# Hand-overs between feed-forward and attention: iterations one after another or woven turns

## What is computed

```python
def fp4_quant_dequant(x):  # blocks of 16 along the last dim
    scale = max(|x|) / 6, at least 1e-12
    q = GRID[searchsorted(MID, |x / scale|)] * sign(x) * scale
def ffn(x):                         # 128 -> 352 -> 128
    h = silu(fp4_linear(x, w_gate)) * fp4_linear(x, w_up)
    return fp4_linear(h, w_down)
def attention(X):                   # T 256, C 128, 16 heads of 8, causal
    A = softmax(mask(Q @ K.T / sqrt(8)))
    return (A @ V) @ Wo + bo
x = x + 0.5 * ffn(layernorm(x))
x = x + attention(layernorm(x))
x = x + 0.5 * ffn(layernorm(x))
```

## Time and profile before

| | us |
|---|---|
| median of 3 runs | 530.16 |
| the profiled execution, its own time | 529.12 |
| its span, first to last instruction | 527.3 |
| busy: PE, DVE, ACT, POOL | 424.6, 429.2, 295.7, 247.9 |

### The profile page before, as it was taken

One profiled execution on the slowest core, in us unless ns is written; L12 is line 12 of the kernel. 1 busy time (PEld: TensorE's weight loads), 2 busy tenths in 40 slices (PEclk: granted clock), 3 DMA queues, 4 the chain that ended last, 5 costly groups with the idle time before them and its releaser, 6 DMA issues.

```text
span 527.3 us, 12678 instructions
## 1 busy us (share of the span) xinstructions
PE 424.6 (81%) x3609; PEld 304.8 (58%) x3625; DVE 429.2 (81%) x1221; ACT 295.7 (56%) x716; POOL 247.9 (47%) x450
## 2 busy tenths in 40 slices
PE   0767777756758999999999998979874878877784
PEld 0435555544636777777777776647542555555564
DVE  5799999998688688888888887587446999999981
ACT  3245555555425677777777776445773355555542
POOL 3354345444514466666666664444542255434521
PEclk9989999999988999999999999789988799999998
DMA  7600000002553444444444445310000000000001
GB/s 213 185 0 3 0 0 0 0 0 66 149 144 102 107 133 134 135 126 122 119 124 129 131 131 134 106 29 5 4 1 1 11 11 20 20 20 19 12 20 31
DMA packets 30525, 35.50 MB, mean 67 GB/s; under 512 B 1683, under 2 KB 27283, under 8 KB 28179
## 3 DMA queue, kind: packets, MB, share of 16 engines
q1 hardware_dynamic: 30483, 34.99, 24.1%
HBM read 21.91 MB, written 10.49 MB: 61 GB/s over the span
## 4 chain that ended last, share of the span: by engine, by line
PE 39%; DVE 32%; issue 16%; ACT 4%; DMA 4%; POOL 2%; DVEq 1%; SPq 1%; ACTq 0%; POOLq 0%
PE bank L1045 7%; PE bank L1017 6%; PE bank L1072 6%; PE bank L1014 4%; DVE hq_amax L675 4%; DVE f_h L805 2%; PE bank L1076 2%; DVE hq_normed L686 2%; DVE hq_grid L709 2%; PE bank L994 2%; DVE hq_odd L692 2%; DVE fln_stats L714 2%; PE bank L956 2%; PE bank L1102 2%; DMA k_stack<-k_parts 2%
## 5 line engine op out<-in xcount | busy, mean ns | idle before, releaser
L836 DVE TENSOR_REDUCE nm<-bank 128x2 f32<-128x512 f32 (+1 forms) x192 | 127.9, 685 | 33.2 <-PE bank L1017 32.4
L618 ACT ACTIVATE probs<-bank 128x512 f32<-128x512 f32 x192 | 113.0, 601 | 64.1 <-PE bank L1045 62.6
L490 POOL TENSOR_SCALAR_AFFINE_SELECT probs<-probs 128x256 f32<-128x256 f32 (+1 forms) x192 | 93.2, 487 | 98.0 <-ACT probs L618 96.6
L1045 PE MATMUL bank<-q_stack,k_stack 75*128 75x256 bf16 (+1 forms) x512 | 75.5, 251 | 6.6 <-ACT probs L618 5.6
L1017 PE MATMUL bank<-k_stack,q_stack 72*128 72x256 bf16 (+1 forms) x512 | 74.8, 248 | 0.9
L924 PE MATMUL bank<-wguT,f_xT 128*128 128x352 f32 x128 | 54.8, 512 | 19.5 <-ACT f_xT L545 18.2
L956 PE MATMUL bank<-wdT,f_hT 128*128 128x128 f32 (+1 forms) x384 | 58.2, 290 | 14.1 <-ACT f_hT L563 14.1
L524 ACT ACTIVATE hq_magic<-hq_exps 128x704 bf16<-128x704 bf16 x32 | 25.3, 790 | 65.3 <-DVE hq_exps L695 65.3
L956 PEld LDWEIGHTS bank<-wdT,f_hT 128*128 128x128 f32 (+1 forms) x384 | 50.3, 200 | 18.7 <-ACT f_hT L563 18.7
L444 POOL TENSOR_TENSOR fln_mean_neg<-fln_mv,minus_one 128x2 f32<-128x2 f32 x32 | 6.3, 198 | 113.0 <-DVE fln_var_eps L725 113.0
L1014 PE MATMUL bank<-causal,ident_bf 128*128 128x256 bf16 (+1 forms) x176 | 54.5, 310 | 0.5 <-DVE nm L836 0.2
(11 more groups left out here) (122 smaller groups left out, 878.5 us busy)
## 6 DMA issues: line engine op xcount, KB each, us to landing
q_stack<-q_parts SPq DMA_DIRECT2D x16, 576.0 KB
k_stack<-k_parts SPq DMA_DIRECT2D x16, 576.0 KB
q_parts<-qk_parts SPq DMA_DIRECT2D x16, 192.0 KB, 2.1
k_parts<-qk_parts SPq DMA_DIRECT2D x16, 192.0 KB, 2.4
v_stack<-zeros_bf SPq DMA_DIRECT2D x1, 2048.0 KB, 10.3
k_parts<-qk_parts SPq DMA_DIRECT2D x16, 128.0 KB, 2.3
out_dram<-x_all SPq DMA_DIRECT2D x16, 128.0 KB, 1.8
q_stack<-nmT SPq DMA_DIRECT2D x16, 24.0 KB
```

The costliest lines, as they stand in the source:

```text
L490: nc.gpsimd.affine_select(out=v, in_=v, compare_op=ALU.is_ge, fill=0.0, base=0, pattern=[[0, heads], [1, P]], channel_multiplier=-1).then_ ...
L618: nc.scalar.activation(probs[:, c, :], ps[:, :], ACT.Exp, scale=SCALE).then_inc(done, 1)
L836: nc.vector.tensor_reduce(nm[:, j, h0:h0 + n], ps[:, :].rearrange("p (h k) -> p h k", h=n), AX_X, ALU.max, negate=True).then_inc(done, 1)
L1045: last = nc.tensor.matmul(ps[:, w * n:w * n + w], k_stack[0:SROWS, s, HG * g + h, k0:k0 + P], q_stack[0:SROWS, s, HG * g + h, q0:T], start ...
```

## The change

The two lists of digits are replaced by lists of turns. A turn names a feed-forward iteration, an attention iteration and an order of steps of both (`f.` for feed-forward's, none for attention's). Steps that don't exist for that iteration are passed over; one iteration may be spread over two turns (feed-forward 2 and 3 of the second hand-over), and assertions in `weave` hold that each step stands there once. The orders of SP's queue stay as they were.

```diff
--- before.py
+++ after.py
@@ -84,15 +84,48 @@
 
 
 FFN1_END = 13
-FFN_TO_ATT = [2, 2, 2, 2, 0, 1, 0, 1, 0, 1, 1]
-
-
-
-TOGETHER = """
-f.xT a.lnN f.lnS f.hq a.xT f.lnA f.lnE f.xq f.gu0 a.xTc f.xr f.hr a.third a.stack f.h0 a.qk f.hT0 a.c1 f.gu1
-a.lnS f.lnN f.hT1 a.split f.dn f.h1 a.lnA a.lnE a.bias a.c2 a.v
-""".split()
-ATT_TO_FFN = [0, 1, 0, 1, 0, 0, 0, 1, 0, 1, 0, 1]
+WARM = """
+third f.xT lnN f.lnS f.hq stack xT f.lnA f.lnE f.xq f.gu0 xTc f.xr f.hr f.h0 qk f.hT0 c1 f.gu1
+lnS f.lnN f.hT1 split f.dn f.h1 lnA lnE bias c2 v
+"""
+FIRST_SCORES = """
+third f.xT lnN f.hq stack xT f.gu0 xTc f.hT0 f.gu1 f.hr f.h0 f.h1 f.hT1 qk c1 S0 S1 f.dn S2 split S3 S4 lnS S5
+c2 S6 lnA S7 lnE S8 bias S9 v S10 S11
+"""
+FIRST_PROBS = """
+nmS third f.hT0 lnN nm S0 f.hT1 S1 xT f.hq xTc f.dn S2 stack f.hr qk ST0 c1 S3 ST1 S4 lnS S5
+ST2 split S6 bias lnA S7 ST3 c2 lnE S8 S9 v ST4 S10 S11
+"""
+FIRST_VALUES = """
+nmS ST5 S0 f.hT0 third  ST6 lnN S1 f.hT1  ST7 nm S2 stack f.dn  ST8 S3 AV0 bias
+ST9 AV1 xT S4  ST10 xTc oc0 lnS S5  ST11 lnA S6 AV2  ST0 lnE S7 qk
+ST1 c1 S8  ST2 split S9 AV3  ST3 c2 oc1 S10 v  ST4 S11
+"""
+FFN_TO_ATT = [(13, 0, WARM), (14, 1, WARM), (15, 2, WARM), (16, 3, WARM), (17, 4, FIRST_SCORES), (18, 5, FIRST_PROBS),
+              (19, 6, FIRST_VALUES), (None, 7, " ".join(ATT_ORDER))]
+LAST_PROJECTION = """
+nmS ST5 S0 AV0 oT0 third  ST6 lnN n0 S1  ST7 nm S2 stack  ST8 S3 AV1 bias
+ST9 oc0 oT1 xT n1 S4  ST10 xTc f.lnS S5  ST11 f.lnA S6 AV2 yT  ST0 yTc f.lnE S7 qk
+ST1 c1 S8 wo  ST2 split S9 AV3  ST3 c2 oc1 wa S10 v f.lnN  ST4 S11
+"""
+LAST_SCORES = """
+nmS ST5 S0 AV0 oT0 third  ST6 n0 S1 f.lnS  ST7 nm S2 stack f.lnA  ST8 S3 AV1 f.lnE
+ST9 oc0 oT1 n1 S4 f.xq  ST10 S5  ST11 S6 AV2 yT f.lnN  ST0 yTc S7
+ST1 S8 wo f.xr  ST2 S9 AV3  ST3 oc1 wa S10 v  ST4 S11
+"""
+LAST_PROBS = """
+nmS ST5 AV0 oT0  ST6 n0  ST7 nm  ST8 AV1  ST9 oc0 oT1 n1 f.xT  ST10  ST11 AV2 yT  ST0 yTc
+ST1 wo  ST2 AV3  ST3 oc1 wa  ST4 f.gu0 f.gu1 f.h0 f.h1
+"""
+LAST_VALUES = """
+ST5 AV0 oT0  ST6 n0  ST7 oT1 n1 f.xT AV1  ST8 yT  ST9 oc0 yTc  ST10 AV2 wo  ST11 f.hq f.xq f.xr f.hr wa AV3 f.gu0 oc1 f.gu1
+f.h0 f.h1
+"""
+LAST_OUTPUT = """
+f.xT f.lnS oT0 f.hq n0 f.lnA f.lnE f.xq f.gu0 oT1 f.xr f.hr n1 f.h0 f.hT0 f.gu1 yT yTc f.lnN f.hT1 wo f.dn f.h1 wa
+"""
+ATT_TO_FFN = [(0, 16, LAST_PROJECTION), (1, 17, LAST_SCORES), (2, 18, LAST_SCORES), (3, 19, LAST_SCORES.replace("f.xq", "").replace("f.xr", "")),
+              (2, 20, LAST_PROBS), (3, 21, LAST_VALUES), (4, 22, LAST_OUTPUT)]
 assert sorted(FFN_ORDER) == sorted(FFN_LAG) and sorted(ATT_ORDER) == sorted(ATT_LAG)
 
 
@@ -183,35 +216,29 @@
 
     ffn1.peeled(range(done, ffn1.start))
     ffn1.loop(eng)
-    hand_over(ffn1, att, FFN_TO_ATT)
+    weave(ffn1, att, FFN_TO_ATT)
     att.loop(eng)
-    hand_over(att, ffn2, ATT_TO_FFN)
+    weave(ffn2, att, ATT_TO_FFN)
     ffn2.loop(eng)
     ffn2.peeled(range(ffn2.end, ffn2.stop))
 
 
-def together(ffn, att, ffn_it, att_it):
-
-
-    assert all(att_it < att.lag[name] for name in att.order if f"a.{name}" not in TOGETHER)
-    for name in TOGETHER:
-        if name[0] == "f":
-            ffn.step(name[2:], ffn_it, ffn_it)
-        else:
-            att.step(name[2:], att_it, att_it)
-
-
-def hand_over(a, b, mix):
-
-    at = [a.end, 0]
-    for n in mix:
-        if n < 2:
-            (a, b)[n].peeled([at[n]])
-            at[n] += 1
-        else:
-            together(a, b, *at)
-            at = [at[0] + 1, at[1] + 1]
-    assert at == [a.stop, b.start]
+def weave(ffn, att, turns):
+
+
+
+    woven = set()
+    for ffn_it, att_it, order in turns:
+        for name in order.split():
+            pipeline, it, step = (ffn, ffn_it, name[2:]) if name.startswith("f.") else (att, att_it, name)
+            if it is not None and 0 <= it - pipeline.lag[step] < pipeline.batches:
+                assert (pipeline is ffn, it, step) not in woven
+                woven.add((pipeline is ffn, it, step))
+                pipeline.step(step, it, it)
+    for pipeline, n in ((ffn, 0), (att, 1)):
+        for it in {turn[n] for turn in turns} - {None}:
+            for step, lag in pipeline.lag.items():
+                assert (pipeline is ffn, it, step) in woven or not 0 <= it - lag < pipeline.batches, (it, step)
 
 
 def macaron_kernel(nc, X, Wq, Wk, Wv, Wo, bo, Wg, Wu, Wd, out):
```

## The result

The changed kernel takes 515.1 us (median of 4 runs, 512.65 to 516.04); the kernel before ran at 529.73 beside it (4 runs, 529.07 to 532.49). The ratio is 0.9728, with a 95% interval of 0.969 to 0.9766. The forecast was 505.6 us with a range of 497 to 515: right in sign, 9.5 us too fast. In the profiled execution the span went from 527.3 to 513.6.

A forecast was written before the change was run, and what follows sets the result against it. Waits between in-order engine queues at the two hand-overs were taken as the loss; gains of 6.2 (first) and 18.4 (second) took 24.6 off 529.12, giving 504.5, or 505.6 us with 1.04 added for the median; range 497 to 515.

The forecast's parts named there:

- turns 15 and 16, third part earlier: First hand-over: POOL's third part at the head of its list shortens DVE's wait by 1.13, twice; 2.2 us gained.
- turn 17: First hand-over: S0 and S1 go ahead of the down projection, but S2 then waits behind it; 0 gained (-0.7 to 2.7).
- turn 18: First hand-over: quantisation behind S1, down projection beneath it, turn at 15.3 us; 3.6 us gained (1.5 to 5.1).
- turn 19: First hand-over: turn of 15.86 us costed at PE's busy time of 15.47; 0.4 us gained.
- turns 16 to 19 of the second: Second hand-over: norms and two quantisations beneath attention's scores, 61.79 us becoming 54.5; 7.3 us gained (3 to 9).
- turn 20: Second hand-over, with feed-forward iteration 2: 14.36 us becoming 12.2; 2.2 us gained (0.5 to 4).
- turn 21: Second hand-over, with iteration 3: quantisation starts after n1, 16.69 us becoming 10.7; 6.0 us gained (3.5 to 7.5).
- turn 22: Second hand-over, with iteration 4: 12.17 us becoming 9.3 by DVE's work; 2.9 us gained (1.5 to 3.6).
- signs: Second hand-over: turns 16 to 19 at 13 to 14 us and full clock; DVE's score waits above 3 us would refute.
- the port rule: Certain VectorE and GpSimd instructions exclude each other; second hand-over's turns 17 and 18 would be 14.3 and 14.2, otherwise 13.5.
- the clock cost the first its gain: Experiments' rival, no chance given: TensorE's clock, not the order, cost the first hand-over its gain.
- The starved-scores rival: Quantisation amid row maxima leaves PE without a bank, clock falls; 7.0 and 3.6 us not gained, 516 us; chance 0.17.

The follow-up runs named there:

- e10: Changed kernel with the gate and up products ahead of AV3 in turn 21; 513.39 us (2 runs).
- e11: Changed kernel with turn 17 one after the other, S0 and S1 earlier in turn 18, gate products ahead of AV3 in turn 21; 506.02 us, ratio 0.958.
- after: The changed kernel itself, both hand-overs woven, against the kernel before; 515.1 us, ratio 0.9728.
- e12: Changed kernel with n0 alone put ahead of the quantisation f.hq in turn 22; 515.95 us (2 runs).
- e9: Changed kernel with attention's output steps, n0 and n1 included, moved ahead of the quantisation in turn 22; 517.32 us (2 runs).
- e3: Changed kernel with POOL's third part and the stack back at their old place in turns 13 to 16; 515.44 us, ratio 0.9731.
- e7: Changed kernel with an earlier second part (c2) and a later bias in WARM, moving the third part onto other DVE steps; 518.02 us (2 runs).
- e4: Changed kernel with turn 17 of the first hand-over written one after the other as before; 511.71 us, ratio 0.9686.
- e8: Changed kernel with turn 18 reordered: S0 and S1 ahead of the maxima's transposes, the copy xTc ahead of f.hq; 512.85 us (2 runs).
- e13: e11 with S2 too put early, ahead of the down projection, in turn 18; 508.23 us, ratio 0.9641.
- e2: First hand-over as changed, second turn by turn as in the kernel before; 531.52 us, ratio 1.0017.
- e5: Changed kernel with turn 18 of the first hand-over one after the other again; 516.88 us, ratio 0.9775 (2 runs).
- e1: First hand-over as in the kernel before, second as changed; 516.0 us, ratio 0.973.

## Why the prediction was wrong

The sum by its steps, gains in us, from the profiled executions:

| step | forecast | measured |
|---|---|---|
| turns 15 and 16, third part earlier | 2.2 | 0.1 |
| turn 17 | 0 (-0.7 to 2.7) | -1.8 |
| turn 18 | 3.6 | 1.0 |
| turn 19 | 0.4 | -0.4 |
| turn 14, same work | 0 | -1.8 |
| turns 16 to 19 of the second | 7.3 | 9.0 |
| turn 20 | 2.2 | 1.7 |
| turn 21 | 6.0 | 4.3 |
| turn 22 | 2.9 | 1.7 |
| all | 24.6 | 13.8 |

The second hand-over was right within its bounds: 16.7 of 18.4. Its signs came too: full clock in turns 16 to 19, and no wait of DVE for scores near 3 us. The sum is closer than its parts, though, since one error helped and three hurt. Turns 16 to 19 came out better, 52.8 against 54.5. I had charged collisions and a halt of the row maxima that hardly show. By the port rule that the prediction cites the two turns would have been 14.3 and 14.2; they are 13.41 and 13.47, near the 13.5 that it gave for the case without. The rule is not refuted (`xq_normed` takes 0.65 and 0.52 there instead of 0.42), but a mask holds POOL for 0.41, the third part for 1.16 and more: a collision costs what is left of the partner, so short partners cost little. Turns 21 and 22 fell short by 1.7 and 1.2 because I costed each at its busiest engine plus a flat sum of waits, and did not follow who stands behind AV3 and behind `f.hq`. e10 and e11 show the first (1.2 and 1.7 back, the latter with turn 22 at after's clock); for the second e12 has 0.5 and e9 the trap.

The first hand-over failed at four of its terms, and at turn 14, which had none.

*The third part* (behind it stands POOL's other work, "which wait for DVE anyway and hide it"). I asked who waits in POOL's queue, and not what runs on DVE at that moment. I had cited the very rule, but only for the second hand-over. The wait went as forecast; e3 shows the same time paid in stretched instructions, 0.1 us gained instead of 2.2, and e7 that with other partners about half of the price comes back.

*Turn 17* ("what is saved ahead of S0 is paid before S2"). The wait did split as I wrote, but the two parts are 0.8 more than the one (0.88 + 1.44 against 1.52), and the same collision adds 0.9 to DVE. e4 has both back: 1.7 us. The order is the cause, the clock being full in both.

*Turn 18* (15.3). The mechanism was possible and the written order was not the one that does it. I gave 0.75 for S0 and 0.75 for the rounding; measured were 1.38, 0.80 and 1.09 of DVE waiting for scores, and 2.32 of PE waiting for `a_xT`. Part is the clock: in e9 the same order ran turn 18 at full clock in 16.39. Of the 1.5 between, 0.4 is the cast at the turn's head (0.62, and 0.18 in e9, where POOL's third part ends at 160.25, as the split begins at 160.21), and 1.1 goes with a clock of 0.90 instead of 1.00 (e4, whose cast takes 0.18 too, took 17.53 at 0.90). The last 1.1 of the 2.6 that are missing go with the order. e8, e11 and e13 then take the queue apart wait by wait, down to 15.41.

*Turn 19* (0.4 gained; 0.4 lost). I costed it by PE. What the profiles show beside it is the third part at its head: the four steps of the split take 1.9 instead of 0.7 of DVE's time, and DVE is busy 11.00 instead of 9.96. No run takes the third part away from there, so this cause is argued, not shown.

*Turn 14* (no term at all). It has nearly the order of before, but took 11.57 with a clock of 0.70 instead of 9.81. Windows of 3 us, the kernel before, then the changed one:

```profile
109.00:112.00 3.00, 0.99 (x5) 0.50 (x4) 2.85 (x13) 1.40 (x3) 1.45 (x4) 1.00 0.00 0
112.00:115.00 3.00, 3.00 (x20) 2.43 (x19) 1.92 (x5) 1.89 (x6) 1.90 (x2) 1.00 0.00 0
```

```profile
109.00:112.00 3.00, 2.09 (x5) 0.74 (x3) 2.93 (x14) 1.48 (x3) 1.03 (x3) 0.50 0.00 0
112.00:115.00 3.00, 3.00 (x8) 2.31 (x9) 1.25 (x4) 0.31 (x2) 2.31 (x3) 0.50 0.00 0
```

The five groups of products from 109 to 112 us keep PE busy 0.99 of 3.00 at full clock and 2.09 at the lower one. The change is not needed for this: e2, e4, e5 and e8 have the changed kernel's instructions up to here, and their turn 14 takes 11.57, 9.81, 9.81 and 9.82, while e1 with the old order takes 11.50. So the rival "the clock cost the first its gain" holds for 1.8 us of turn 14 and about 1.1 of turn 18, and falls for turn 17 and for the third part.

The starved-scores rival (516) named the right time by half a mechanism: turns 17 and 18 of the second hand-over stayed at full clock and gave their whole gain, and where the clock did fall, in turn 18 of the first, it was not by `f.hq`. PE's products are at the lower level from 160 to 163 us, at S0, S1 and the first half of the down projection, after the 2.37 us in which PE waited for the split; `f.hq` begins on DVE at 162.81, and PE's wait of 2.32 behind it lies at full clock. Nor does the length of the wait for the split decide it: it was 1.12 both in e9 (turn at 1.00) and in e12 (0.76). That the time came out near 516 is luck for this rival. My range ended at 515 since I thought all bad ends together unlikely; in the first hand-over three of the terms came out near or beyond their bad ends (0.1, -1.8 and 1.0 against 0, -0.7 and 1.5), and turn 14 had no bad end at all. (By the bounds as written all bad ends leave 9.7, not 9.2; it changes nothing.)

Open: e11's median lies 5.7 us under e4's, but their profiled executions differ by only 1.8: turns 20 to 22 give 1.8, the first distance takes 1.2 back (e11's turn 15 fell), and 1.1 lie ahead of turn 13, where both kernels have the same instructions. How much of the rest is order and how much the clock isn't settled. Nor is which of e11 and e13 is the faster.

## What to carry to other kernels

When a step is moved to the head of a turn, look at what the other engines execute at that very moment, not only at who waits for it; a freed wait can come back as longer instructions, and a busy share that grows while the turn stays the same is its sign. In a queue in order, cost a woven turn wait by wait (what stands directly ahead of each instruction, on every engine that its chain crosses), not by the busiest engine plus a flat sum. Where free banks can be filled before a long block of products, fill them all, so that their consumer has work meanwhile (in e13 all three; its share in the gain is not told from the clock's). Where whole times differ by less than chance, compare turn by turn, and only turns at the same clock.

## What the runs showed of the hardware

The spread of the executions goes with TensorE's granted clock. Of the 38 executions of the kernel before that ran beside the experiments, those with a mean granted clock of 0.971 took 524.8 to 525.46 us, with 0.964 527.32 to 528.75, with 0.961 (one) 529.1, with 0.958 529.29 to 530.31, with 0.949 532.48 to 532.88, and the one with 0.936 took 536.56. That is 3.3 us for each 0.01. Others show it less cleanly: e11's six runs go from 505.02 at 0.993 to 510.06 at 0.98, but e2 took 532.41 at 0.945 and 532.5 at 0.958. A change of 1 us can't be seen in two such times, but it can in the turns, where most lengths agree within 0.02 us from one kernel to the next (turns 16 to 19 of the second hand-over: 52.79 in after, 52.79 in e4, 52.77 in e11).

Which stretches fall differs between executions of the same instructions: one and the same order of turn 18 ran at 1.00, 0.90 and 0.76 in e9, e4 and e12, and took 16.39, 17.53 and 19.24 us. The orders of turns 20 to 22 are after's in e3, where they took 38.21 with turns 21 and 22 at a clock of 0.86 and 0.70, and 35.92 in after at 1.00 and 0.84.
